# A dummy product in front of every second shifted product of the first attention

## The reference, cut to what matters

```
def _masked_softmax(dots, allow):
    logits = jnp.where(allow, dots, neg)
    rowmax = jnp.max(logits, axis=-1, keepdims=True)
    unnorm = jnp.where(allow, jnp.exp(logits - rowmax), 0.0)
    denom = jnp.sum(unnorm, axis=-1, keepdims=True)
    return unnorm / jnp.where(denom == 0, 1.0, denom)
...
qkv = x @ w_qkv
...
dots = jnp.einsum('bhnd,bhmd->bhnm', q, k) * scale
allow = jnp.tril(jnp.ones((n, n), dtype=bool), k=-1)
attn = _masked_softmax(dots, allow)
out = jnp.einsum('bhnm,bhmd->bhnd', attn, v)
...
return out @ w_out + b_out
```

## Time and profile before

| | us |
|---|---|
| median of 3 runs | 1000.91 |
| the three runs | 995.64, 1001.81, 1000.91 |
| the profiled execution, its own time | 996.52 |
| its span from the first to the last instruction | 994.8 |
| mean granted clock of TensorE, share of 2.4 GHz | 0.950 |

### The profile page before, as it was taken

One profiled execution on the slowest core, in us unless ns is written; L12 is line 12 of the kernel. 1 busy time (PEld: TensorE's weight loads), 2 busy tenths in 40 slices (PEclk: granted clock), 3 DMA queues, 4 the chain that ended last, 5 costly groups with the idle time before them and its releaser, 6 DMA issues. The chain is left out here.

```text
span 994.8 us, 19429 instructions
## 1 busy us (share of the span) xinstructions
PE 894.2 (90%) x6145; PEld 608.8 (61%) x6145; DVE 729.0 (73%) x2048; ACT 630.5 (63%) x1410; POOL 536.7 (54%) x664
## 2 busy tenths in 40 slices
PE   7999999889999999989898999999999998974297
PEld 5444444444678888876566576657666755654297
DVE  5676777773798999984997778868985889436064
ACT  2565656555678888854776677777877766841064
POOL 4234637243604433200667877787868768960544
PEclk9999999995999999999999999999999989995599
DMA  4000001000344335122000000000000000022330
GB/s 140 1 1 1 23 1 45 1 24 0 115 152 113 115 121 126 50 63 61 1 2 1 2 1 2 2 1 2 1 2 1 2 1 2 1 72 121 118 115 21
DMA packets 28859, 40.36 MB, mean 41 GB/s; under 512 B 3452, under 2 KB 18321, under 8 KB 28640
## 3 DMA queue, kind: packets, MB, share of 16 engines
q1 hardware_dynamic: 26832, 36.03, 11.9%
q0 software_dynamic: 1504, 3.17, 1.0%
q10 hardware_dynamic: 432, 0.01, 0.0%
HBM read 32.87 MB, written 6.79 MB: 40 GB/s over the span
## 5 line engine op out<-in xcount | busy, mean ns | idle before, releaser
L1515 POOL TENSOR_SCALAR probs<-probs,rinv 128x128 f32<-128x128 f32 (+3 forms) x256 | 273.8, 1085 | 97.7 <-DVE rinv L1378 97.6
L1448 ACT ACTIVATE probs<-probs,rowmin 128x128 f32<-128x128 f32 (+3 forms) x256 | 142.1, 555 | 51.0 <-DVE rowmin L1372 50.5
L1372 DVE CUSTOM_DVE_ANT_0 probs<-psum,adj 128x128 f32<-128x128 f32 (+3 forms) x256 | 122.4, 478 | 64.6 <-PE psum L1230 64.0
L842 ACT ACTIVATE pT<-psum 128x1024 f32<-128x1024 f32 (+3 forms) x128 | 89.6, 702 | 63.2 <-PE psum L598 62.1
L1230 PE MATMUL psum<-k_sb,q_sb 64*128 64x256 f32 (+3 forms) x512 | 104.9, 487 | 17.4 <-DVE rowmin L1372 17.2
L770 DVE TENSOR_REDUCE top<-psum 128x2 f32<-128x256 f32 (+3 forms) x128 | 102.5, 818 | 21.0 <-PE psum L578 20.8
L1457 ACT ACTIVATE pt<-psum 128x128 f32<-128x128 f32 (+3 forms) x256 | 108.3, 424 | 8.7 <-PE psum L1240 8.5
L1240 PE MATMUL psum<-ident,probs 128*128 128x128 f32 x640 | 99.2, 279 | 3.6 <-ACT pt L1457 2.3
L1823 ACT ACTIVATE r_hid<-psum,b1t 128x512 f32<-128x512 f32 x125 | 82.7, 689 | 30.6 <-PE psum L1662 26.8
L1240 PEld LDWEIGHTS psum<-ident,probs 128*128 128x128 f32 x640 | 74.5, 141 | 45.0 <-POOL probs L1515 22.6
L901 POOL TENSOR_SCALAR_AFFINE_SELECT pT<-pT 128x512 f32<-128x512 f32 x64 | 40.8, 637 | 111.4 <-ACT pT L842 111.3
(11 more groups left out here) (307 smaller groups left out, 1912.0 us busy)
## 6 DMA issues: line engine op xcount, KB each, us to landing
r_share<-shares SPq DMA_DIRECT2D x12, 1024.0 KB, 7.1
s_wall<-in_w_all SPq DMA_DIRECT2D x1, 4624.0 KB, 13.7
sorted_x<-blank SPq DMA_DIRECT2D x1, 2967.0 KB, 12.1
s_xg<-sorted_x SPq DMA_DIRECT2D x23, 129.0 KB, 2.9
r_w1s<-in_w SPq DMA_DIRECT2D x16, 128.0 KB, 5.8
r_w2s<-in_w SPq DMA_DIRECT2D x16, 128.0 KB, 6.1
r_share<-shares SPq DMA_DIRECT2D x6, 256.0 KB, 3.4
r_share<-shares SPq DMA_DIRECT2D x2, 768.0 KB, 5.1
```

Of the source, the lines that this page charges most:

```text
L842: act.activation(pT[:, c % PR:c % PR + 2, 0:W], psum[:, e_bank(c):e_bank(c) + 2, 0:W], ACT.Exp).then_inc(exped, 1)
L1372: dve.tensor_tensor_reduce(probs[:, k, 0:K], s_bank[h][:, 0:K], adj[:, OFF[i]:OFF[i] + K], 1.0, FLOOR, ALU.add, ALU.min, rowmin[:, k:k + 1 ...
L1448: act.activation(probs[:, k, 0:K], probs[:, k, 0:K], ACT.Exp, bias=rowmin[:, k:k + 1], scale=-1.0, accum_out=rsum[:, k:k + 1]).then_inc(ex ...
L1515: pool.tensor_scalar(probs[:, k, 0:K], probs[:, k, 0:K], rinv[:, k:k + 1], None, ALU.mult).then_inc(normed, 1)
```

## The change

In `pe_shift`, behind the waits and in front of the shifted product, each even item c gets a product that nobody reads, in the first 128 columns of the bank that the shifted product then overwrites: up to c = 216 one bf16 product of `ident_b` with itself, from c = `BARE` = 218 on one product of `pe_warm` (fp32). No wait is added, and nothing is taken away.

```diff
                 ENDING = NS - ITEMS
+                BARE = NS - ITEMS - LAG
...
                     if c >= 2:
                         pe.wait_ge(exped, (c if c < ENDING + 2 else c - 2) // 2)
+                    if c % 2 == 0:
+                        if c >= BARE:
+                            pe_warm(pe, banks[e_bank(c)], 1)
+                        else:
+                            pe.matmul(banks[e_bank(c)][:, 0:P], ident_b[:], ident_b[:], start=True, stop=True,
+                                      skip_group_check=True)
                     pe.matmul(banks[e_bank(c) + c % 2][:, 0:W], kst[rows, U % 3, kb * P:(kb + 1) * P], q2[rows, U % 2, kb * P:N],
                               start=True, stop=True).then_inc(shifted, 1)
```

## The result

The changed kernel takes 1159.8 us (median of four runs, 1139.47 to 1171.01) against 1000.69 us before. The forecast was 1018 us in a range of 1000 to 1036, 22 us above the execution that it started from: the direction was right, and the 159 us measured are seven times that size.

A forecast was written before the change was run, and what follows sets the result against it. TensorE was taken to bound the first attention. 26 us for broken rounds plus 5 for fp32 dummies minus 9 for the clock made +22 us on the profiled 996.52 us, so 1018 us, range 1000 to 1036.

The forecast's parts named there:

- The bound: First attention, 39 to 211 us: TensorE is the bound, booked busy 156.23 of 172.00 us.
- The round breaks: Double steps: four products running together become a score alone, a dummy and a round of three; 0.345 us each in 97.
- the price of the breaks at full clock: First attention: 45 us of added TensorE time, 19 us of it hidden in idle time, so 26 us remain.
- The rounds that wait: 12 of 109 double steps: the shifted product already waits for an exponential, so only the dummy's 0.105 us is added.
- The price of a dummy: Even shifted products up to c = 216: one bf16 dummy costs 0.105 us by itself, from two mask products in 0.21 us.
- The clock: Granted TensorE clock in the attention: kept up through the last unit, winning 9 us; smaller falls counted at nothing.
- more falls of the clock: Rival, attention: scores alone make falls frequent, a tenth of 180 us at half clock, some 9 us more; 1027 to 1040; chance 0.08.
- The clock in the last unit: Last unit and tail, 219.60 to 246.40 us: dummies keep the clock up, 9 us come back (bounds 0 and 13.4).
- The two terms for the end, +5 and -9 us: Last unit and behind the last scores: 19 fp32 dummies cost about 5 us, the kept clock returns 9 us.
- the last unit's clock fell all the same: Rival, last unit: the 9 us don't come back, fp32 dummies run at half clock; +35 us, 1031 us; chance 0.25.
- the round that does not break: Rival, double steps: the score streams on beside the dummy's loading, only 0.105 us paid; 986 to 992 us; chance 0.09.
- the small price between: Rival, double steps: about 0.2 us a step, no change that can be told, within 1%; chance 0.08.

The follow-up runs named there:

- the run with the round parted in the middle: To the kernel before: both scores, a 16-column bf16 dummy up to c = 216, then both shifted products; no fp32 dummies. 1044.45 us, ratio 1.0469.
- the run that fills the wait: To the kernel before: two fp32 dummies in front of each whole round of double steps 246 to 254, in a free bank. 989.01 us, ratio 0.990.
- the longer exponentials: To the kernel before: ScalarE computes the first of each pair of exponentials twice in 109 double steps; whole rounds, no dummy. 1012.48 us, ratio 1.015.

## Why the prediction was wrong

**The bound** was read rightly: TensorE sets the pace of this stage, and it does so all the more behind the change.

**The round breaks**: right, and as the weighed rule of the Trainium skill ("TensorE: Matmul & The Clock Gate", Part 3, "The mechanism") has it. The trace after agrees: the dummy's weights are loaded from 41.34 us on, 0.25 us behind the score's begin and just ahead of the dummy. The unit at full clock was forecast at some 15.3 us and is 15.0 in the one interval that shows it; the price of the breaks at full clock, forecast as 26 us, is 24 us in the run with the round parted in the middle, which breaks it at another place. The rounds that wait are 11 in the trace, not 12, which changes the sum by 0.3 us.

**The price of a dummy**: too low. A bf16 one between products of 32 rows takes 0.16 us from begin to begin (41.35 to 41.51), not 0.105. The prediction halved the 0.21 us of two mask products, and the halves differ: before, the second mask begins 0.07 us behind the first (113.46 us in the earlier trace rows), and the score at 113.67 us 0.14 us behind the second:

```profile
113.53 0.22 PE L570 MATMUL psum<-pen_rest,ident_b 128*128 128x128 bf16 x1
```

So a full product in front of one of 32 rows costs about 0.15 us. Over 109 dummies that is 6 us, little beside the 159.

**The clock**: this is the step that failed. The sum kept the clock up through the last unit and counted the lesser falls at nothing ("more work for TensorE speaks for its going, a round that keeps only 32 rows at work speaks against"). The second half of that sentence was the result. It came back as a rival, "more falls of the clock", with a chance of 0.08 and a size of one tenth of the stage, while in the trace it is 343 of some 400 us. The mistake was to read a fall as a short event, as the one before 39 us in the earlier trace rows is. With whole rounds it ends; with every round broken it mostly does not, as the run with broken rounds in seven units shows (some 3 us against 170 from the same place). Of the 174 us some 24 are the breaks, if they cost what the round parted in the middle does; nearly all of the rest, some 150, is by difference the half clock.

The row that should have warned of it is in the earlier trace rows: in the 26.80 us of the slow stretch TensorE was booked busy for 25.27 us and stayed slow. The prediction weighed it for the last unit alone, and did not ask what a stage full of such time would do.

**The clock in the last unit**: the 9 us were a fair size (the run that fills the wait gains 7 us), but a dummy behind the wait does not bring them. The two terms for the end, +5 and -9 us, stand against +12 us in the run with the fp32 dummies alone.

**The rivals**: the last unit's clock fell all the same, as one of them said; the round that does not break and the small price between are refuted by the timeline.

**What stays open**: what starts a fall. Broken rounds ran at full clock for as little as 6 us (broken rounds in seven units) and 20 us (the changed kernel), and for as much as 167 us (the round parted in the middle), before one came, and there is one profiled execution of each kernel. That it is the small number of rows at work, rather than the time lost, is made likely by the runs with the round parted in the middle (0.65 us for the width that takes 0.68 in the changed kernel, and yet a clock that held for longer) and with the longer exponentials, but not settled.

## What to carry to other kernels

Products that use a part of the rows and run side by side are one unit of work: a product on all rows, or a wait of TensorE for one of them, goes in front of it or behind it, never between. A dummy product helped the clock here where it took the place of standing still, in front of a wait and in a bank of its own (7 us won), and not behind the wait (12 us lost). Where a change thins out the work of an engine whose clock depends on work, the price is to be taken for the whole stage at the lower clock as well, and compared with the trace's own stretches there.

## What was not expected of the hardware

A TensorE that is booked busy without a gap can stay at 1.2 GHz for hundreds of microseconds: 320.50 of 320.50 us in the changed kernel, 162.00 of 162.00 in the one with broken rounds in seven units, where the clock was back 6 us behind the last of them. The Trainium skill ("TensorE: Matmul & The Clock Gate", Part 1, "What's actually happening") has activity release the slow clock; these rows do not agree, if activity is read as booked busy time. The profile's busy share did not tell here whether the clock would hold.
